# Matmuls of ones in three pauses of TensorE, in a fused decoder layer

## What is computed

```
x = x + self_attention(layernorm(x))        # 16 heads of 16, keys and values rebuilt from a latent of 64
x = x + cross_attention(layernorm(x), ctx)  # 64 context rows
x = x + moe(layernorm(x))

# self-attention: scores clipped, multiplied by a decay of the distance, softmax
scores = clip(q @ k.T / 16) * exp(-1e-4 * abs(i - j))

# moe: a shared MLP for all 2048 tokens, and 16 experts of which each token takes its best 2
shared = (silu(xf @ Sg) * (xf @ Su)) @ Sd
probs  = softmax(xf @ Wr); topk_p, topk_i = top_k(probs, 2)
y     += topk_p * (silu(xf @ wg) * (xf @ wu)) @ wd     # for the chosen experts only, in the kernel
```

## Time and profile before

| | us |
|---|---|
| median of 3 runs | 605.74 |
| the three runs | 603.89, 605.74, 606.75 |
| profiled execution, its own time | 607.95 |
| span of it, first to last instruction | 606.2 |
| outside the span | 1.75 |
| mean granted TensorE clock | 0.970 |
| PE busy | 545.2 (90%) |
| DVE, ACT, POOL busy | 375.0, 392.6, 213.3 |

### The profile page before, as it was taken

One profiled execution on the slowest core, in us unless ns is written; L12 is line 12 of the kernel. 1 busy time (PEld: TensorE's weight loads), 2 busy tenths in 40 slices (PEclk: granted clock), 3 DMA queues, 4 the chain that ended last, 5 costly groups with the idle time before them and its releaser, 6 DMA issues.

```text
span 606.2 us, 14134 instructions
## 1 busy us (share of the span) xinstructions
PE 545.2 (90%) x4519; PEld 294.9 (49%) x4520; DVE 375.0 (62%) x1001; ACT 392.6 (65%) x568; POOL 213.3 (35%) x238
## 2 busy tenths in 40 slices
PE   3995999999999999999999899999988889899970
PEld 2452333333333333333356677777554666666640
DVE  5897565556556655655644587888858634444564
ACT  4577989999999999999972556445243723333310
POOL 4000792495049500000003432452265614444450
PEclk9997999999999999999998999999989979999995
DMA  9923334444444444444406600000022234334846
GB/s 259 365 97 71 67 71 75 75 78 78 77 78 78 78 78 78 77 78 78 94 29 190 193 9 2 3 1 1 18 93 82 87 98 138 122 121 130 260 157 208
DMA packets 53595, 60.20 MB, mean 99 GB/s; under 512 B 10769, under 2 KB 44690, under 8 KB 53554
## 3 DMA queue, kind: packets, MB, share of 16 engines
q1 hardware_dynamic: 46546, 46.19, 32.0%
q0 software_dynamic: 3792, 10.36, 4.8%
q10 hardware_dynamic: 3216, 3.15, 1.6%
HBM read 22.17 MB, written 18.61 MB: 67 GB/s over the span
## 4 chain that ended last, share of the span: by engine, by line
PE 70%; DVE 10%; DMA 5%; issue 5%; ACT 4%; SPq 4%; POOL 2%; DVEq 1%; another core or an unknown queue 1%; ACTq 0%; POOLq 0%
PE ps L715 19%; PE ps L726 19%; PE ps L1102 9%; PE ps L1119 4%; DMA x_slots<-val,place_i 3%; PE ps L859 2%; PE ps L759 2%; PE ps L1094 2%; PE ps L927 2%; SPq L414 2%; SPq L412 2%; DVE ftmp L1773 2%; PE ps L642 1%; PE ps L877 1%; DMA qT<-y_tok 1%
## 5 line engine op out<-in xcount | busy, mean ns | idle before, releaser
L1632 DVE TENSOR_TENSOR ps<-ps,kstack 128x128 f32<-128x128 f32 (+3 forms) x256 | 123.2, 493 | 96.7 <-PE ps L715 96.5
L1255 ACT ACTIVATE pT<-ps 128x1024 f32<-128x1024 f32 x128 | 125.3, 1036 | 5.5 <-PE ps L715 2.3
L715 PE MATMUL ps<-qstack,kstack 96*128 96x512 bf16 x352 | 92.8, 387 | 5.7 <-ACT kstack L1244 3.9
L726 PE MATMUL ps<-pT,vcur 128*32 128x256 f32 x1024 | 80.4, 386 | 0.0
L1255 ACT ACTIVATE xn<-ps 128x1024 f32<-128x1024 f32 x64 | 65.8, 1028 | 7.7 <-PE ps L715 7.4
L592 POOL DMA_INDIRECT y_tok<-ftmp,dest_i x47 | 45.1, 959 | 61.2 <-DVE ftmp L2051 60.4
L1255 ACT ACTIVATE xnT<-ps 128x1024 f32<-128x1024 f32 x64 | 65.9, 1030 | 0.7 <-DVE ps L1632 0.6
L1102 PE MATMUL ps<-parts,xnT 128*128 x188 | 54.6, 416 | 6.2 <-issue 6.1
L715 PEld LDWEIGHTS ps<-qstack,kstack 96*128 96x128 bf16 x352 | 27.4, 98 | 63.9 <-issue 31.3
L1432 ACT ACTIVATE oT<-ps 128x128 f32<-128x128 f32 x47 | 13.0, 277 | 63.7 <-PE ps L1102 52.4
L565 POOL TENSOR_TENSOR resid<-resid,projb 128x512 f32<-128x512 f32 x8 | 10.1, 1264 | 114.0 <-DVE xn L1966 113.4
(11 more groups left out here) (296 smaller groups left out, 946.3 us busy)
## 6 DMA issues: line engine op xcount, KB each, us to landing
qstack<-parts SPq DMA_DIRECT2D x132, 64.0 KB, 2.3
x_slots<-wcur SPq DMA_DIRECT2D x1, 6016.0 KB, 21.1
kT<-x_slots SPq DMA_DIRECT2D x47, 128.0 KB
kstack<-parts SPq DMA_DIRECT2D x132, 32.0 KB, 2.0
early<-parts SPq DMA_DIRECT2D x60, 64.0 KB, 2.3
resid<-in_x_dram SPq DMA_DIRECT2D x4, 512.0 KB, 5.2
parts<-in_L_ffn_Wg_dram SPq DMA_DIRECT2D x16, 128.0 KB, 2.3
parts<-in_L_ffn_Wu_dram SPq DMA_DIRECT2D x16, 128.0 KB, 2.3
```

The lines of the kernel that those rows point to most:

```text
L715: nc.tensor.matmul(ps[:, score_bank(g3, kt) + g, :], kstack[g3][:, kt * P:(kt + 1) * P], qstack[g3][:, 1 - first, 512 * g:512 * (g + 1)], ...
L726: mm = nc.tensor.matmul(out_g, vcur[:, r, kt, :], pT_ring[kt % 4].rearrange("p (t g q) -> p g t q", g=4, q=2 * HD)[:, g, :, :], start=(kt ...
L1255: nc.scalar.activation(pT_ring[kt % 4], two_banks(score_bank(g3, kt)).rearrange("p a n -> p (a n)"), ACT.Exp, bias=-SHIFT).then_inc(s_exp, 1)
L1632: nc.vector.tensor_tensor(blk, blk, within[:, side, 4 * P - n:] if side == 0 else within[:, side, 0:n], ALU.mult)\
```

## The change

A helper `keep_busy(n, target)` is added. It issues n bf16 matmuls of `ones_bf` (128x128, all ones) with itself, broadcast to the width of the target, into a PSUM bank that nobody reads then. It is called at five places: ahead of the last `norms`, behind it, and ahead of the wait for the flag (5, 2 and 12 matmuls of 512 columns, bank 0); between `gate_up(1, 1)` and `counts(1)` (7 of 512 columns, bank 5); and between `destinations()` and the first tile's transposes (20 of 256 columns, bank 7). Their results are overwritten later. The calls set no semaphore and wait for none.

```
@@ in the block of TensorE, behind norms()
+            def keep_busy(n, target):
+                columns = target.shape[-1]
+                for _ in range(n):
+                    nc.tensor.matmul(target, ones_bf[:], ones_bf[:].unsqueeze(1).to_broadcast([P, columns // P, P]),
+                                     start=True, stop=True)
@@ ahead of the path's decision
             mm.then_inc(s_cT_ps, 1)
+            keep_busy(5, ps[:, 0, :])
             norms(NCHUNK - 1)
+            keep_busy(2, ps[:, 0, :])
             pe.wait_ge(s_kmean, 1)
             nc.tensor.matmul(ps[0:2 * HD, 4, 0:B * KD], head_ind[:], ksq[:].rearrange("p b k -> p (b k)"),
                              start=True, stop=True).then_inc(s_kmean, 1)
+            keep_busy(12, ps[:, 0, :])
             pe.wait_ge(s_cT, 2)
@@ ahead of the second counts
             gate_up(1, 1)
+            keep_busy(7, ps[:, 5, :])
             counts(1)
             down(0)
@@ ahead of the first tile
             destinations()
+            keep_busy(20, ps[:, 7, 256:])
```

## The result

| | before | changed |
|---|---|---|
| median of 20 runs, us | 606.0 | 608.3 |
| lowest and highest | 603.23, 609.25 | 605.11, 611.83 |
| ratio, 95% interval | | 1.0044 (1.0028 to 1.0060) |
| profiled execution, its own time | 607.95 | 605.11 |
| its span, mean granted clock | 606.2, 0.970 | 603.4, 0.980 |

The changed kernel is slower by 2.3 us by the medians and by 2.7 by the ratio. That is under the 0.5% that were called no change, but the interval leaves out 1.0, and 608.3 lies outside the range given. The profiled executions say the opposite, 2.8 us faster: that of the changed kernel is the fastest of its 20, and that of before, at 607.95, is slower than 17 of the 20 runs of before. Executions of one kernel differ by 6 us, more than the whole effect.

The account below looks back on a forecast made before the run. The prediction blamed half clock after PE's pauses at the head of attention, second counts and first tiles. From the median 605.74 us, terms 0, -0.5 and -2.0 gave 603.2 us, range 600.9 to 606.2.

Parts of the forecast that it names:

- Third place: First tiles, behind destinations: full clock gains 2.9 us with the transposes, lower bound 2.0, carried by the chain.
- Hidden with 0.7 us to spare: The 20 fills ahead of the first tile end at 486.7; its transposes start only at 487.39.
- The term of -2.0: Gain taken for the first tiles against the median, the lower bound of that place.
- slower rival: First tile: fills at half clock or destinations over 0.7 us later make transposes 1.4 us late; 607.1 us, 6%.
- Second place: The second counts and down(0): DVE's places start earlier with the clock up; bounds 0 and 1.45 us, 0.5 taken.
- gain of 0.5: Second counts: saving if DVE's 3.63 us idle ahead of the places hangs on the low clock.
- hidden by DVE's choices: The 7 fills ahead of the second counts take 1.5 us of a 2.4 us pause and cost nothing.
- the remaining pauses: What the fills leave of PE's pauses, 1.3, 0.9 and 0.7 us, shorter than the harmless 2.0 us.
- First place: Head of attention: PE leads by 1.0 to 1.4 us but waits it away on SP's queue; 0 taken.
- the lead: Head of attention: PE reaches head 1 1.0 to 1.4 us earlier, given back by head 7 at 114.30.
- the rival at 25%: First tile: transposes don't count as PE-busy, a 2.3 us gap lowers the clock anyway; 605.0 us, 25%.
- The gain of 2.9 us: First tiles: 2.5 us from tile 0 to tile 3 at full clock, 2.9 with the transposes.

Follow-up runs that it names:

- e12: The kernel before, unchanged, measured against itself as a control, which gave a second profile of it: 606.68 us, ratio 0.9998.
- e1: Changed kernel with only the fills of 5, 2 and 12 matmuls around the last norms and the flag: 607.54 us, ratio 1.0008 to before.
- e2: Changed kernel with only the 7 matmuls ahead of the second counts: 608.94 us, ratio 1.0036 to before.
- e4: Changed kernel without the 20 matmuls ahead of the first tile's transposes: 609.78 us, ratio 1.0042 to before.
- e13: Repeat of e8, only 7 matmuls of 128 columns ahead of the second counts: 607.71 us, ratio 1.0032 to before.
- e5: Changed kernel with only the 7 matmuls ahead of the second counts, plus 9 between gate_up(0, 2) and gate_up(1, 2): 605.46 us, ratio 1.0001 to before.
- e6: Kernel before plus only 9 matmuls between gate_up(0, 2) and gate_up(1, 2): 605.08 us, ratio 1.0005 to before.
- e8: Changed kernel with only the 7 matmuls ahead of the second counts, narrowed to 128 columns: 605.73 us, ratio 1.0005 to before.
- e18: As e8 but with 28 matmuls of 128 columns ahead of the second counts: 607.02 us, ratio 1.0019 to before.
- e17: Changed kernel without the 7 matmuls ahead of the second counts; 5, 2, 12 and 20 stay: 605.68 us, ratio 1.0012 to before.
- e16: Kernel before without POOL's 16 scatters of the first 1,024 tokens, so part of the computation is missing: 603.49 us beside 606.33, a single run.
- e10: Repeat of e2, unchanged, only the 7 matmuls ahead of the second counts: 609.16 us, ratio 1.0042 to before.
- e14: As e5 but with 24 matmuls in place of 9 between gate_up(0, 2) and gate_up(1, 2): 605.40 us, ratio 1.0006 to before.
- e15: Changed kernel with only the fill ahead of the first tile, 40 matmuls in place of 20: 608.12 us, ratio 1.0022 to before.
- e3: Changed kernel with only the 20 matmuls ahead of the first tile: 607.98 us, ratio 1.0023 to before.
- e7: Changed kernel, all fills kept, with 40 matmuls in place of 20 ahead of the first tile: 607.53 us, ratio 1.0036 to before.
- e11: The changed kernel itself, measured again: 609.98 us, ratio 1.0055 to before.

## Why the prediction was wrong

**Third place: the step that failed** is "This stands on the chain with nothing beside it", and "Hidden with 0.7 us to spare". Both were true of the execution profiled, but not of the kernel. Its pause of 2.93 us between `destinations` and the transposes is 0 in five profiles with a late signal (e12, e1, e2, e4, e13), because there PE is the late one. The term of -2.0 had to be 0 or above there. Its gain isn't there, tiles 0 to 3 take 4.9 to 5.1 us without fills, and the fills stand on the chain with 2.18 us. This is the slower rival's mechanism, `destinations` over 0.7 us later (1.2 us in the changed kernel's profile, 485.68 against 484.46); the half clock wasn't needed, nor a second delay. Where the signal is prompt, the wait is there and longer, 4.0 to 5.6 us in e5, e6, e8 and e18, and 20 fills are too few for it (e17). The size was wrong as well: at full clock tile 0 to tile 3 takes 4.9 us and not 4.0, so that even before's own execution had 1.6 us to give and not 2.5. What the third place costs in time isn't settled: 1.0023 and 1.0022 alone, with 1.0 just inside both intervals, and almost nothing on top of the others (1.0044 against 1.0042).

**Second place: the other step that failed**, and by the ratios the larger. "If that idle of DVE hangs on the low clock ... then the change removes it": it doesn't hang on it (2.94 us late at clock 1.00), but on POOL's scatters, as far as e16 shows. So the gain of 0.5 isn't there. Its premise, the 5.36 us of `down(0)`, was a feature of the execution too, since six of eight profiles without the fill have 3.67. That the 7 fills are "hidden by DVE's choices" holds only where the pause ahead of the counts is long: before's second profile has 0.86 us there, and the fills take 1.67.

Why the second place costs 1.9 to 2.5 us (e2, e10 and e13, 0.32 to 0.42% of 606) is not shown. Three ways are open.

- The pause behind. The sentence that "the remaining pauses ... are all shorter than the 2.0 us that did no harm" looked only at the pauses that the change fills. In the changed kernel's profile the next one is 2.9 us, and `gate_up(1, 2)` takes 5.13 us and not 3.60, with nothing beside it. The column "to dest." has the price of such a loss: 24.08 at full clock, 25.5 to 27.1 where some 3 to 6 us of low clock lie behind DVE's product. Filling that pause too brings the ratio back to 1.0006 (e14). Against it: the intervals of e14 and e13 overlap; e13's seven narrow matmuls should have cost little; and e12, e1 and e15 lose the clock there without any fill, so that on average the fill adds 0.4 us. If before usually loses that clock, e14, which keeps it, should have been faster than before, and it isn't. The pause filled without the second place where the signal is late would test this; e6 had a prompt signal.
- A later signal. From the first scatter to the places on DVE it is 18.3 us on average over before, e12, e1, e3 and e15 (17.4, 18.9, 19.0, 19.0, 17.4), and 19.3 over the eight late profiles with fills at the second place (16.3 to 21.9), in steps of some 1.4 us, the pace of POOL's scatters. That is 1.0 us, more than the 0.4 of the clock, but with so few executions it is a hint.
- The fills in PE's way, the 0.5 us by which the counts end later in four of the eight. e14, which has it, is at 1.0006.

What is shown is that the second place alone costs time where the signal is late (e2 and e10, both intervals clear of 1.0).

**First place: right about the sum.** The term was 0, and e1 reads 1.0008. The clock is 1.00 from 54.0 to 60.8, the 12 end at 55.25 and the flag is there at 55.32. The first eight scores take 2.50 us, not 3.59 and not the forecast 1.9, because PE waits 0.4 and 0.1 us among them for ACT's exponentials; the lead of 1.1 us is in the range that the prediction gave. Head 7 started at 113.53 and not 114.30. The prediction called itself wrong "if head 7 starts over 0.5 us earlier", so by its own words that part missed; but one pair of executions can't carry it. Head 7 starts at 113.7 to 115.8 in the 13 profiles without these fills (mean 114.7) and at 113.5 to 115.3 in the seven with them (mean 114.5). The lead is given back. PE's waits for loads moved from `kstack` to `early`, 2.0 us in all and not 3.

Something else happens behind it. From head 7's first score to the end of the last score it is 196.09 us in ten of those 13 profiles (196.3 to 197.2 in e2, e10 and e15), and 196.5 to 197.3 in all seven with fills at the first place; heads 8 and 9, for example, take 8.05 and 8.36 us in the changed kernel's profile, where a head takes 7.88. That is 0.4 to 1.3 us that the term of 0 didn't have, too little for e1's interval to tell. Its cause stays open.

**The rule of the rival at 25%.** The changed kernel's fill ran into the transposes without a gap (487.86), and the clock stayed 1.00 through them and the tiles. So the pause from 486.7 to 489.0 that the rival needed wasn't there, and its rule wasn't tested. The Trainium skill, "TensorE: Matmul & The Clock Gate", Part 4, says that a transpose doesn't count as PE-busy in the way a matmul does; the 1.6 us of transposes here, between fills and dense matmuls, are no test of it. The nearest to one is e7, where 1.3 us of standing still and 1.8 us of transposes follow each other and the clock stays at 1.00; but a pause of 3.27 us (e3) did no harm either, so it decides nothing.

**The sum and the range.** The terms were 0, -0.5 and -2.0 us; measured alone, as a share of 606 us, they are +0.5 (e1), +2.2 (e2) and +1.4 us (e3), the first and the last with 0 in their intervals, and 4.1 in sum against the 2.7 of all together. The gain of 2.9 us was cut to 2.0 since the profile lay 2.2 us above the median. That sign should have said more: the third place was worth that much in this execution, and no second one was there to say whether it usually is. The range, which ended at 606.2, gave the slower rival too little room: it took a late `destinations` for an exception, and in 12 of the 13 profiles with a late signal it ended over 0.7 us later than in before's.

None of the kernels that compute the whole layer beats the kernel before. The closest are e5, e6, e8 and e14, at 1.0001 to 1.0006.

## What to carry to other kernels

Matmuls that nobody reads can hold the clock up, but that pays only where PE is what the others wait for at the pause's end. At the first place they worked in all seven profiles, and the lead went to SP's queue. PE can also come sooner to the next wait that another engine ends, so look at the pause behind the change, not only the one it fills.

Where executions of one kernel lie 1% apart, one profile shows one of several chains. Three things that this prediction priced were gone in before's second profile: the slow `down(0)`, the long pause ahead of the counts, and the wait for the first tile. Take a wait or a stretch of low clock as the kernel's own only if a second profile has it too; that profile costs one run of the kernel before.

## What the runs showed of the chip

- Signals of PE reached DVE 2.3 to 7.9 us after the matmul in 13 of the 19 profiles of kernels that keep all scatters, whatever the clock, and in 0.04 us in the others. Which of the two it was went by the comparison, each on its chip: in the first, third and fourth always late, in the second and fifth never. Without POOL's 16 scatters of the first half it was 0.04 us on a chip that was otherwise late. How the scatters hold up a signal between two other engines stays open.
- Pauses of PE of 2.0 us (before) left the clock at 1.00, those of 2.5 us (e11) and 2.9 us (changed) did not, and one of 3.27 us (e3) did. The length of the pause alone doesn't decide.
- In e12 the clock fell at 442.7 although PE had stood still for no longer than 0.46 us since 430; just before it had made 8 transposes (L956, 1.30 us) and 16 matmuls of 16 columns (L967, 1.96 us). Before's first profile has the same work there and kept 1.00.
- Matmuls of ones do hold the clock up: between 52 and 66 us it stays at 1.00 in all seven profiles with the fills at the first place, and reads 0.50 for 6.8 or 10.2 us in all 13 without them. At the second place no such thing is shown.
